# Four attention layers on one core: key sums, parts of the row maxima and late roots given to other engines

## The chip, the core and the metric

The kernel runs on one core of a Trainium2 chip. A core has TensorE (PE in the rows; its weight loads are PEld), VectorE (DVE), ScalarE (ACT), GpSimd (POOL), and SyncE (SP), which issues most DMAs. The engines run their own instruction streams and meet at semaphores: an instruction may wait until a counter has reached a value, and raises one when it ends. The metric is the device time of the kernel in microseconds (us), lower is better.

## The reference

One activation x of 16 batches x 128 x 256 goes through four layers in turn. What matters here, cut from the code:

```
L0: two cross-attentions (16 heads of 128) with layer norms, then a feed forward
L1: q = Wq x + bq;  k = Wk kv + bk;  v = Wv kv + bv;  attn = softmax(where(kv_mask, q k, -inf))
    mean = attn v;  std = sqrt(relu(attn v*v - mean*mean))
    xn = (x*m - sum(x*m)/n_valid) / sqrt(relu(var) + 1e-5);  out = (xn * std + mean) * m
L2: masked self-attention, masked cross-attention, feed forward with gelu, each with a layer norm
L3: q = layer_norm((x + pos)^T);  kv = layer_norm((ctx + pos)^T)
    r = softmax(Q K^T / sqrt(8)) V Wo + q
    out = (gelu(layer_norm(r) W1 + b1) W2 + b2 + r)^T
```

L1 and L3 have 16 heads over 256 queries and 256 keys for each batch, so that one head has a score matrix of 256 x 256.

## The kernel before

The program is one block with a stream for each engine, written by hand. Each layer is a function that exists once for every engine. In order of time: layer 0 (`wide`), feed forward 0, layer 1, layer 2, feed forward 1, layer 3 and its last feed forward (`feed_forward3`).

**Packed attention.** Layers 1 and 3 run the same code, `attention(third, ...)`, in windows, one for each batch n, and each window has 16 steps j, one for each head. A window works on several batches: the core of batch n (exponentials and weighted sums), the scores and row maxima of batch n+1 (`following`), the projections of n+2 (`ahead`), the keys and norms of n+3 (`coming`) and, in layer 3, the row statistics of batch n+4 (`fourth`). Steps that all engines take in each window:

- TensorE makes the scores of a head (L1074) for the next batch; VectorE takes their maximum over the keys, negated (`tensor_reduce`, L2106, 16 a window). The scores of head j wait for the reduce of head j-3.
- After 8 heads the maxima are brought to the rows of the next matmuls: each is split into a rounded part and a rest (`split_maxima`, L2067 and L2068), the parts are transposed by TensorE (`turn_maxima`, L1054), VectorE copies the result (`copy_maxima`, L2074) and DMAs put it behind the queries. The first half of batch n+1 is turned at j=9, the second half of batch n at j=1.
- TensorE makes the shifted scores of batch n (L1083), ScalarE their exponentials (L1672), TensorE the sums with the values (L1103).

TensorE's stream is in order, so the turn stands in front of the heads that follow:

```
pe.wait_ge(s.max_split, 2 * m + half + 1)
pe.transpose(spare[quad[0], 0:P], max_parts[half]..., ident[:, :]).then_inc(s.max_turned, 1)
```

VectorE's copy stands in front of the reduce of head 9 and waits for this transpose. Late in the window, at j=13, TensorE puts the queries of the batch after in place (`put`, L1061), and waits there for VectorE's copy of the values (`v_taken`, L2379, j=12).

**Layer 1's keys.** GpSimd casts the mask of a batch (L2612). VectorE sums the masked keys with one pass that also writes the product (L2169) and multiplies the sum by one over the valid count (L2173, `key_mean`). GpSimd subtracts the mean (L2630), multiplies by the mask (L2631), and adds the mean (L2643) into `keys_in`, which the projection of the keys reads (L1122).

**Layer 3's norms.** VectorE aggregates the statistics of 4 groups of rows (L2396, step j=6). GpSimd makes the inverse root from them by Newton's method in 14 instructions, each of which waits for the one before it (L2687, L2688, then L2690 to L2693 three times), and normalizes with four `tensor_scalar` (L2697). It then adds the positions to the rows of later batches (L2674, L2676). GpSimd does this root in 13 windows, i = -1 to 11 where i counts layer 3's batches; the first three batches are done by VectorE.

**Feed forward.** VectorE's loop over 8 rounds makes the low part of the hidden layer (`hidden_lows`, L2020), the low part of the next input (`input_low`, L2014), the norm of the one after (`norm`) and adds. In feed forward 1 `begin_last` (L2321 to L2326) stands ahead of that loop: it scales layer 3's query weights and fills the two buffers `vn`, and raises `packed_ready`.

**Last feed forward.** VectorE takes statistics of 8 groups of rows, makes their inverse root in 11 instructions (L266 to L272), and normalizes (`normalize3`, L2419), in 4 turns.

Of the kernel before, what the change touches and what calls it, by code (L numbers as in the profile page):

```python
# [152 lines left out]
class Packed:  # L153
# [3 lines left out]
    def __init__(self, sem, name):  # L157
# [32 lines left out]
        self.key_summed = sem(f"{name}_key_summed")  # L190
# [34 lines left out]
SQUARES = (9, 11)  # L225
PLACED_ROWS, TURNED_BACK, HEADS = (9, 10), (13, 14), (13, 14)
# [7 lines left out]
RSTD_STEPS = 2 + 3 * 4  # L234
# [255 lines left out]
def program(nc, t, out, outer):  # L490
# [12 lines left out]
    minus_half = sbuf(outer, "minus_half", [P, 4])  # L503
# [153 lines left out]
    scratch_keys, scratch_values = hidden[:, 4, :], hidden[:, 5, :]  # L657
# [139 lines left out]
    block = outer.enter_context(nc.Block())  # L797

# [626 lines left out]
    def _(act):  # L1425
# [179 lines left out]
        def attention(third, q_bias, k_bias, when, conclude=None):  # L1605
# [11 lines left out]
            def window(n, at, u=None):  # L1617
# [3 lines left out]
                for j in range(HN):  # L1621
# [46 lines left out]
                    if core:  # L1668
# [121 lines left out]
    def _(dve):  # L1790
# [203 lines left out]
        def feed_forward(which, bias):  # L1994
# [53 lines left out]
        def attention(third, q_bias, k_bias, when, release, own, conclude):  # L2048
# [11 lines left out]
            def split_maxima(m, half):  # L2060

                parts = max_parts[half]
                whole = maxima[half][:, :, :, :].rearrange("p a g w -> p a (g w)")
                after(dve, s.max_turned, 2 * m + half - 1)
                dve.wait_ge(s.max_ready, HN * m + HALF_HEADS * (half + 1))
                chain = Chain(dve, s.prep_chain, 2 * m + half)
                chain.link(dve.tensor_copy(parts[:, :, 0, :], whole))  # L2067
                dve.tensor_tensor(parts[:, :, 1, :], whole, parts[:, :, 0, :].bitcast(F32), ALU.subtract).then_inc(s.max_split, 1)  # L2068
# [7 lines left out]
            def window(n, at, u=None):  # L2076
                u = n % SLOTS if u is None else u
                core, following, carry, ahead = (at(i) is not None for i in (0, 1, -1, 2))
                for j in range(HN):
                    if core and j == TURN_MAXIMA[1] - 1:  # L2080
# [10 lines left out]
                    if following and j == TURN_MAXIMA[0] - 1 and third:  # L2091
                        split_maxima(n + 1, 0)
# [24 lines left out]
        def layer1():  # L2117
# [41 lines left out]
            def own(n, at, u, j):  # L2159
                following, carry, ahead, coming = (at(i) is not None for i in (1, -1, 2, 3))  # L2160
# [3 lines left out]
                if coming and j == 3:  # L2164
                    dve.wait_ge(s.loaded[1 - u], pair_turn(0, at(3), 1 - u))
                    after(dve, s.in_ready, n + 3)
                    dve.wait_ge(s.keys_chain, 3 * (n + 3) + 1)
# [741 lines left out]
```

## Time and profile before

| | us |
|---|---|
| median of 3 runs | 2293.92 (2293.31 to 2295.13) |
| the profiled execution: its own time | 2298.61 |
| the profiled execution: span of the trace | 2296.9 |
| TensorE busy | 2171.5 (95%) |
| VectorE busy | 1563.9 (68%) |
| ScalarE busy | 1574.0 (69%) |
| GpSimd busy | 739.7 (32%) |

Layer 0 takes up to about 1100 us, feed forward 0 to 1170, layer 1 to 1458 (a window of 16.5 us), layer 2 to 1841, feed forward 1 from 1847 to 1960, layer 3 from 1961 to 2257 (a window of 17.0 us), its last phase from 2246 to the end. The granted clock is at 0.9 or more of full speed in most of the 40 slices of the page. The busy time of TensorE includes time in which a matmul stands in the pipeline, so that a share near 100% does not mean that no instruction waits. In a timeline each row is one instruction, or some of one kind in a row: start, busy time, engine, line, operation, output and inputs, and in brackets how long the engine was idle before and what released it.

### The profile page before, as it was taken

To read this page: it belongs to the slowest core of one execution; us is meant where nothing else is said; L and a number is where in the kernel's file an instruction comes from. 1 tells how busy PE (TensorE), PEld (TensorE's weight loads), DVE (VectorE), ACT (ScalarE), POOL (GpSimd) and SP (SyncE) were. 2 spreads that over 40 slices of the span, in tenths; PEclk is the share of its full clock that TensorE was granted. 3 is DMA by queue.
4 is the path that set the end of the run, shared out by engine and by line. 5 is a ranking of instruction groups with operands and counts; after the bars stand their busy time and mean duration, and the time that the engine had idled before them with its cause. 6 is when DMAs were issued, how large, how long until landed. Compare 5 with 4: busy or idle time off the path is not lost. (4 is left out here: it accounts for less than half of the span.)

```text
span 2296.9 us, 51674 instructions
## 1 busy us (share of the span) xinstructions
PE 2171.5 (95%) x17289; PEld 1762.8 (77%) x17289; DVE 1563.9 (68%) x3980; ACT 1574.0 (69%) x4478; POOL 739.7 (32%) x1037
## 2 busy tenths in 40 slices
PE   6999999999999999997989999789999989899998
PEld 5899999998999999997975666456666679666664
DVE  6655555557555555557658999687777666799986
ACT  4666666665667667665737777577778866488874
POOL 2211111123211111103024655377777620344310
PEclk9999999999999999999979999799999999799999
DMA  5101112010001000002000000100000000000001
GB/s 134 24 24 24 24 24 60 24 24 1 24 24 24 24 24 24 1 1 73 0 8 10 12 9 6 38 8 1 6 17 19 10 8 6 6 10 11 8 4 38
DMA packets 72943, 47.12 MB, mean 21 GB/s; under 512 B 29232, under 2 KB 71600, under 8 KB 72752
## 3 DMA queue, kind: packets, MB, share of 16 engines
q1 hardware_dynamic: 70288, 43.30, 7.2%
q8 instruction: 114, 1.87, 0.3%
q10 hardware_dynamic: 2464, 1.32, 0.3%
q14 instruction: 77, 0.63, 0.1%
HBM read 41.45 MB, written 2.10 MB: 19 GB/s over the span
## 5 line engine op out<-in xcount | busy, mean ns | idle before, releaser
L2106 DVE TENSOR_REDUCE maxima<-bank 128x2 f32<-128x512 f32 x512 | 332.8, 681 | 34.7 <-PE bank L1083 32.3
L1672 ACT ACTIVATE probs_t<-bank 128x512 f32<-128x512 f32 x512 | 282.5, 601 | 67.2 <-PE bank L1074 66.0
L1966 DVE SCALAR_TENSOR_TENSOR wide_heads_low<-bank,wide_columns,wide_heads_high 128x128 fp32r<-128x128 f32 x512 | 155.7, 346 | 210.1 <-ACT wide_heads_high L1537 210.1
L1525 ACT ACTIVATE wide_probs<-bank,wide_neg_max 128x129 f32<-128x129 f32 x512 | 184.2, 365 | 117.7 <-DVE wide_neg_max L1946 113.4
L2461 POOL TENSOR_TENSOR wide_columns<-wide_pair_columns,zero 128x8 f32<-128x8 f32 x16 | 3.4, 210 | 648.7 <-DVE x L1979 638.8
L1520 ACT ACTIVATE wide_probs_t<-bank 128x256 f32<-128x256 f32 x256 | 98.4, 384 | 161.7 <-PE bank L945 159.7
L1950 DVE RECIPROCAL wide_inverse<-wide_sums 128x2 f32<-128x2 f32 x256 | 42.4, 166 | 227.8 <-ACT wide_probs L1525 227.8
L1531 ACT ACTIVATE wide_probs<-wide_probs,wide_inverse 128x128 f32<-128x128 f32 x448 | 156.0, 396 | 52.0 <-DVE wide_inverse L1950 52.0
L1083 PE MATMUL bank<-k_packed,q_packed 32*128 32x256 f32 x1024 | 176.5, 344 | 3.7 <-ACT q_packed L1657 2.2
L1074 PE MATMUL bank<-q_packed,k_packed 32*128 32x256 f32 x1024 | 170.8, 337 | 8.3 <-ACT probs_t L1672 7.6
L1709 ACT ACTIVATE probs<-scores_masked,neg_max 128x128 f32<-128x128 f32 x512 | 163.2, 394 | 10.6 <-DVE neg_max L2285 9.8
L959 PEld LDWEIGHTS bank<-wide_probs_t,wide_v 128*128 128x128 f32 x1024 | 148.0, 190 | 26.3 <-ACT wide_probs_t L1520 10.1
L1074 PEld LDWEIGHTS bank<-q_packed,k_packed 32*128 32x128 f32 x1024 | 107.0, 190 | 77.1 <-ACT probs_t L1672 39.3
L803 PE MATMUL bank<-wide_weights_high,wide_heads_high 128*128 128x256 f32 x512 | 166.0, 324 | 0.0
L959 PE MATMUL bank<-wide_probs_t,wide_v 128*128 128x128 f32 x1024 | 157.1, 276 | 4.8 <-ACT wide_probs_t L1520 4.7
L935 PE MATMUL bank<-wide_k,wide_q 128*128 128x129 f32 x1024 | 156.1, 275 | 2.1 <-POOL wide_normed_low L2487 1.6
L1537 ACT ACTIVATE wide_heads_high<-bank,wide_columns 128x128 fp32r<-128x128 f32 x512 | 155.4, 353 | 1.5 <-PE bank L959 0.8
L803 PE MATMUL bank<-wide_weights_high,wide_ctx_high 128*128 128x256 f32 x512 | 148.2, 289 | 0.0
L935 PEld LDWEIGHTS bank<-wide_k,wide_q 128*128 128x128 f32 x1024 | 139.9, 190 | 8.7 <-POOL wide_normed_low L2487 2.2
L805 PE MATMUL bank<-wide_weights_high,wide_heads_low 128*128 128x256 f32 x512 | 144.4, 282 | 0.0
L804 PE MATMUL bank<-wide_weights_low,wide_heads_high 128*128 128x256 f32 x512 | 144.3, 282 | 0.0
L1103 PE MATMUL bank<-probs_t,vn 128*32 128x256 f32 x2048 | 143.0, 398 | 1.2 <-DVE max_rows L2074 0.6
(316 smaller groups left out, 6794.5 us busy)
## 6 DMA issues: line engine op xcount, KB each, us to landing
cn<-in_ctx SPq DMA_DIRECT2D x48, 128.0 KB, 2.1
q_packed<-max_rows SPq DMA_DIRECT2D x256, 4.0 KB
wide_pair_weights<-in_L_xattn_wq SPq DMA_DIRECT2D x15, 256.0 KB, 2.8
wide_pair_weights<-in_L_xattn_wk SPq DMA_DIRECT2D x15, 256.0 KB, 3.1
wide_pair_weights<-in_L_xattn_wv SPq DMA_DIRECT2D x15, 256.0 KB, 3.7
wide_pair_weights<-in_L_xattn_wo SPq DMA_DIRECT2D x15, 256.0 KB, 3.5
x<-in_x SPq DMA_DIRECT2D x4, 512.0 KB, 10.3
wide_ctx_rows<-in_ctx SPq DMA_DIRECT2D x4, 512.0 KB, 8.8
```

The source lines that it names most:

```text
L803: pe.matmul(acc, wh, mh, start=start, stop=False)
L935: last = pe.matmul(wide_scores[b % 2][:, h * KEYS0:(h + 1) * KEYS0], q0[k % 2][:, h, b * P:(b + 1) * P], k0[k % 2][:, h, b, :], start=True ...
L959: last = pe.matmul(wide_heads[a % 2][:, h * P:(h + 1) * P], v0[parity][:, a, h * P:(h + 1) * P], probs_t0[:, a, h, :], start=True, stop=True)
L1074: last = pe.matmul(shifted_bank[j % 2][:, c * D:(c + 1) * D], k_packed[u][quad[a], pack, c * P:(c + 1) * P], q_packed[u][quad[a], pack, :] ...
L1083: last = pe.matmul(head_scores[packed_scores(1 - u, j)][:, c * D:(c + 1) * D], q_packed[1 - u][quad[b], pack, c * P:(c + 1) * P], k_packed ...
L1525: last = act.activation(probs0[:, b, h, :], wide_scores[b % 2][:, h * KEYS0:(h + 1) * KEYS0], ACT.Exp, bias=neg_max0[:, b, h:h + 1], accum ...
L1531: last = act.activation(probs0[:, b, h, 0:P], probs0[:, b, h, 0:P], ACT.Copy, scale=inverse0[:, b, h:h + 1])
L1537: last = act.activation(heads_high[:, h, a, :], wide_heads[a % 2][:, h * P:(h + 1) * P], ACT.Identity, bias=columns[slot][:, 3, h:h + 1])
L1672: act.activation(probs_t[j % 8][:, :], shifted_bank[j % 2][:, :], ACT.Exp, bias=0.0).then_inc(s.exp_ready, 1)
L1709: last = act.activation(probs[t][:, part], scores_masked[t][:, part], ACT.Exp, bias=neg_max[t][:, h:h + 1])
L1966: last = dve.scalar_tensor_tensor(heads_low[:, h, a, :], wide_heads[a % 2][:, h * P:(h + 1) * P], columns[slot][:, 3, h:h + 1], heads_high ...
L2106: dve.tensor_reduce(maxima[pack // 2][:, b, pack % 2, :], head_scores[packed_scores(1 - u, j)][:, :].rearrange("p (a k) -> p a k", a=UNITS ...
```

## The change

- **Layer 1's key sum.** VectorE's product with sum and its multiplication are gone. GpSimd multiplies keys and mask (`masked_keys`) right behind the cast of the mask; ScalarE runs `masked_keys` through an Identity with the scale one over the valid count and an accumulated sum, at j=4, behind the exponentials of that step. GpSimd's three steps that follow become two: (mask - 1) * mean, and `masked_keys` less that.
- **Layer 3's maxima.** `split_maxima` leaves VectorE. GpSimd takes the second half of batch n as the first thing in its window, and the first half of batch n+1 behind the root and the first of the four `tensor_scalar` of the norm, or where the window has no root, by itself.
- **Layer 3's root** on GpSimd becomes an addition and one power over 128x4.
- **Last phase.** VectorE's root over 128x8 becomes an addition on VectorE and a power on GpSimd (`roots3`), for which VectorE waits ahead of `normalize3`.
- **Feed forward.** The first round of VectorE's loop is written out ahead of it, in both feed forwards of this form, and `begin_last` stands behind that round.

```diff
+KEY_MEAN = 4
-RSTD_STEPS = 2 + 3 * 4
+RSTD_STEPS = 2
-    minus_half = sbuf(outer, "minus_half", [P, 4])
+    minus_half = sbuf(outer, "minus_half", [P, 8])
+    def parts_of_maxima(engine, m, half, apart=False):
+        s = packed
+        parts = max_parts[half]
+        whole = maxima[half][:, :, :, :].rearrange("p a g w -> p a (g w)")
+        after(engine, s.max_turned, 2 * m + half - 1)
+        engine.wait_ge(s.max_ready, HN * m + HALF_HEADS * (half + 1))
+        if apart:
+            engine.sem_inc(idle, 1)
+        chain = Chain(engine, s.prep_chain, 2 * m + half)
+        chain.link(engine.tensor_copy(parts[:, :, 0, :], whole))
+        engine.tensor_tensor(parts[:, :, 1, :], whole, parts[:, :, 0, :].bitcast(F32), ALU.subtract).then_inc(s.max_split, 1)
@@ ScalarE, attention, behind the exponential of step j
+                    if coming and not third and j == KEY_MEAN:
+                        if isinstance(n, int):
+                            act.wait_ge(packed_ready, 2)
+                        act.wait_ge(s.keys_masked, n + 4)
+                        act.activation(scratch_keys, masked_keys, ACT.Identity, scale=valid[:, ds(at(3), 1)],
+                                       accum_out=key_mean[:, 0:1]).then_inc(s.key_mean, 1)
@@ VectorE, feed forward
             input_low(0)
             norm(1)
+            hidden_lows(0)
+            input_low(1)
+            norm(2)
+            add(0)
             if which:
                 begin_last()
-            with dve.Fori(0, ROUNDS - 2) as i:
+            with dve.Fori(1, ROUNDS - 2) as i:
@@ VectorE, attention
-                    if core and j == TURN_MAXIMA[1] - 1:
+                    if core and j == TURN_MAXIMA[1] - 1 and not third:
                         split_maxima(n, 1)
-                    if following and j == TURN_MAXIMA[0] - 1 and third:
-                        split_maxima(n + 1, 0)
-                    dve.tensor_tensor_reduce(scratch_keys, cn[1 - u][:, :], mask_row[:, 0, :], 1.0, 0.0, ALU.mult, ALU.add, key_sum[:, 0:1])\
-                       .then_inc(s.key_summed, 1)
-                    dve.tensor_tensor(key_mean[:, :], key_sum[:, :], valid[:, ds(at(3), 1)], ALU.mult).then_inc(s.key_mean, 1)
@@ VectorE, last phase
-            row_statistics(dve, chain, [bank[h][:, m * P:(m + 1) * P] for h in range(SLOTS) for m in range(4)], stats3, idle)
+            moments(dve, chain, [bank[h][:, m * P:(m + 1) * P] for h in range(SLOTS) for m in range(4)], stats3, idle)
+            dve.tensor_scalar(stats3.shifted[:, :], stats3.mean_var[:, :, 1], EPS, None, ALU.add).then_inc(ff.chain, ROOT_STEPS)
+            dve.wait_ge(n2.root_ready, 2 * B + r + 1)
@@ GpSimd, layer 1
-                    keys.mark(pool.tensor_copy(mask_row[:, 0, :], row(mask_bytes, at(3))))
+                    keys.link(pool.tensor_copy(mask_row[:, 0, :], row(mask_bytes, at(3))))
+                    pool.wait_ge(s.loaded[1 - u], pair_turn(0, at(3), 1 - u))
+                    pool.tensor_tensor(masked_keys, cn[1 - u][:, :], mask_row[:, 0, :], ALU.mult).then_inc(s.keys_masked, 1)
-                    keys.link(pool.tensor_scalar(scratch_keys, cn[1 - u][:, :], key_mean[:, 0:1], None, ALU.subtract))
-                    keys.link(pool.tensor_tensor(scratch_keys, scratch_keys, mask_row[:, 0, :], ALU.mult))
+                    keys.link(pool.tensor_scalar(scratch_keys, mask_row[:, 0, :], ones[:, 0:1], key_mean[:, 0:1], ALU.subtract, ALU.mult))
-                    pool.tensor_scalar(keys_in[1 - u], scratch_keys, key_mean[:, 0:1], None, ALU.add).then_inc(s.in_ready, 1)
+                    pool.tensor_tensor(keys_in[1 - u], masked_keys, scratch_keys, ALU.subtract).then_inc(s.in_ready, 1)
@@ GpSimd, layer 3
+                if core:
+                    parts_of_maxima(pool, n, 1, True)
                     step(pool.tensor_scalar(shifted, stats.mean_var[:, :, 1], EPS, None, ALU.add))
-                    step(pool.tensor_scalar(rstd.bitcast(I32), shifted.bitcast(I32), -0.5, 1597463007.0, ALU.mult, ALU.add))
-                    for _ in range(3):
-                        step(pool.tensor_tensor(work, rstd, rstd, ALU.mult))
-                        step(pool.tensor_tensor(work, work, shifted, ALU.mult))
-                        step(pool.tensor_scalar(work, work, -0.5, 1.5, ALU.mult, ALU.add))
-                        step(pool.tensor_tensor(rstd, rstd, work, ALU.mult))
+                    step(pool.tensor_tensor(rstd, shifted, minus_half[:, 0:4], ALU.pow))
                     for k in range(4):
                         ins = pool.tensor_scalar(norm_packed[u]..., ALU.subtract, ALU.mult)
+                        if following and k == 0:
+                            parts_of_maxima(pool, n + 1, 0, True)
                     ins.then_inc(s.rows_normed, 1)
+                elif following:
+                    parts_of_maxima(pool, n + 1, 0, True)
+        def roots3():
+            norm_two = 2 * SLOTS + ROOT_STEPS
+            for r in range(TURNS3):
+                pool.wait_ge(ff.chain, 2 * ROUNDS * (norm_two + 1) + (statistics_steps(8) + 6) * r + statistics_steps(8))
+                pool.tensor_tensor(stats3.rstd[:, :], stats3.shifted[:, :], minus_half[:, :], ALU.pow).then_inc(n2.root_ready, 1)
```

GpSimd's order in a window of layer 3, before the change (`mean_var` are the statistics, `rstd` the inverse root, `w_qkv` is the memory that holds the rows; L2690 to L2693 come three times, of which one stands here):

```order
L2687 TENSOR_SCALAR stat_shifted<-mean_var 128x4
L2688 TENSOR_SCALAR rstd<-stat_shifted 128x4
L2690 TENSOR_TENSOR stat_work<-rstd 128x4
L2691 TENSOR_TENSOR stat_work<-stat_work,stat_shifted 128x4
L2692 TENSOR_SCALAR stat_work<-stat_work 128x4
L2693 TENSOR_TENSOR rstd<-rstd,stat_work 128x4
...
L2697 TENSOR_SCALAR w_qkv<-w_qkv,mean_var,rstd 128x128 x4
L2674 TENSOR_TENSOR w_qkv<-x,positions 128x256
L2676 TENSOR_TENSOR w_qkv<-cn,positions 128x256
```

And in the changed kernel, where L810 and L811 are the parts of the maxima:

```order
L810 CAST max_parts<-maxima 128x4x4
L811 TENSOR_TENSOR max_parts<-maxima,max_parts 128x4x4
L2685 TENSOR_TENSOR w_qkv<-x,positions 128x256
L2687 TENSOR_TENSOR w_qkv<-cn,positions 128x256
L2698 TENSOR_SCALAR stat_shifted<-mean_var 128x4
L2699 TENSOR_TENSOR rstd<-stat_shifted,minus_half 128x4
L2703 TENSOR_SCALAR w_qkv<-w_qkv,mean_var,rstd 128x128
L810 CAST max_parts<-maxima 128x4x4
L811 TENSOR_TENSOR max_parts<-maxima,max_parts 128x4x4
L2703 TENSOR_SCALAR w_qkv<-w_qkv,mean_var,rstd 128x128 x3
```

The 14 steps have become two, and the parts of the first half of the next batch, on which the turn waits, stand behind the power and one norm step. VectorE's order around this turn was:

```order
L2396 BN_AGGR mean_var<-stat_sums 128x2 x4
L2057 TENSOR_TENSOR k_low<-bank,k_high 128x256
L2106 TENSOR_REDUCE maxima<-bank 128x2
L2374 RECIPROCAL inverse<-bank 128x16
L2045 TENSOR_TENSOR heads_out<-bank,inverse 128x128
L2067 CAST max_parts<-maxima 128x4x4
L2068 TENSOR_TENSOR max_parts<-maxima,max_parts 128x4x4
L2106 TENSOR_REDUCE maxima<-bank 128x2
L2074 CAST max_rows<-bank 32x128
L2106 TENSOR_REDUCE maxima<-bank 128x2
```

In the changed kernel the same stretch of VectorE, by its new line numbers, is:

```order
L2402 BN_AGGR mean_var<-stat_sums 128x2 x4
L2081 TENSOR_TENSOR k_low<-bank,k_high 128x256
L2122 TENSOR_REDUCE maxima<-bank 128x2
L2380 RECIPROCAL inverse<-bank 128x16
L2069 TENSOR_TENSOR heads_out<-bank,inverse 128x128
L2122 TENSOR_REDUCE maxima<-bank 128x2
L2092 CAST max_rows<-bank 32x128
L2122 TENSOR_REDUCE maxima<-bank 128x2
```

The two rows that make the parts are gone from between the reduces of head 7 and head 8, and the copy (L2092) keeps its place. At the start of feed forward 1, VectorE's rows were, with the loop's branch as the fifth:

```order
L1815 TENSOR_SCALAR norm_rows<-x,mean_var,rstd 128x256 x2
L1824 TENSOR_TENSOR x<-x,row_bias 128x512
L2321 TENSOR_SCALAR w_queries<-w 128x128
L2323 MEMSET vn 128x1024 x2
L2326 MEMSET vn 128x32 x2
L2026 UNCONDITIONAL_BRANCH
L2026 ISA
L2020 TENSOR_TENSOR hidden_low<-hidden,hidden_high 128x512
```

Now the low parts follow the norm at once, and the fill comes behind the round's end:

```order
L1844 TENSOR_TENSOR x<-x,row_bias 128x512
L2040 TENSOR_TENSOR hidden_low<-hidden,hidden_high 128x512 x4
L2034 TENSOR_TENSOR hidden_in_low<-hidden_in,hidden_in_high 128x512
L1822 BN_STATS stat_sums<-x 128x6 x2
...
L1844 TENSOR_TENSOR x<-x,row_bias 128x512
L2029 TENSOR_TENSOR x<-x,bank 128x512
L2327 TENSOR_SCALAR w_queries<-w 128x128
L2329 MEMSET vn 128x1024 x2
L2332 MEMSET vn 128x32 x2
```

The scaling and the four fills, which stood ahead of the first low parts, are now behind the whole first round.

## Rows read from the trace of the kernel before

**Rows 1.** Busy time by stretch: us, PE, PEld, DVE, ACT, POOL, PEclk, DMA share, GB/s.

```profile
2057.17:2074.13 16.96, 16.52 (x175) 10.80 (x175) 15.60 (x40) 13.59 (x30) 7.30 (x21) 1.00 0.03 10
```

**Rows 2.** Waits of layer 3's windows (1987 to 2260 us): total, times, longest.

```profile
POOL stat_shifted L2687 <- DVE mean_var L2396: 84.4, 12, 8.4
PEld bank L1074 <- ACT probs_t L1672: 20.0, 66, 0.7
```

**Rows 3.** Timeline of GpSimd in one window of layer 3.

```profile
2064.27 0.23 POOL L2687 TENSOR_SCALAR stat_shifted<-mean_var 128x4 f32<-128x4 f32 x1 [6.88 <-DVE mean_var L2396]
2069.86 3.15 POOL L2697 TENSOR_SCALAR w_qkv<-w_qkv,mean_var,rstd 128x128 f32<-128x128 f32 x4 [0.37 <-POOL rstd L2693]
```

**Rows 4.** Timeline of VectorE, same window.

```profile
2056.08 0.66 DVE L2068 TENSOR_TENSOR max_parts<-maxima,max_parts 128x16 fp32r<-128x16 f32 x1
2063.70 0.37 DVE L2396 BATCH_NORM_AGGREGATE mean_var<-stat_sums 128x2 f32<-128x6 f32 x4
2064.29 0.68 DVE L2106 TENSOR_REDUCE maxima<-bank 128x2 f32<-128x512 f32 x1
2065.58 0.18 DVE L2068 TENSOR_TENSOR max_parts<-maxima,max_parts 128x16 fp32r<-128x16 f32 x1
2066.42 0.28 DVE L2074 CAST max_rows<-bank 32x128 fp32r<-32x128 f32 x1
2068.90 0.41 DVE L2379 COPY vn<-bank 128x256 f32<-128x256 f32 x1
```

**Rows 5.** Timeline of TensorE, same window.

```profile
2066.01 0.27 PE L1054 MATMUL bank<-ident,max_parts 128*32 128x128 f32 x1
2069.48 0.38 PE L1061 MATMUL bank<-q_high,place 128*128 128x256 f32 x1
```

**Rows 6.** Lines of GpSimd: two powers and a 128x16 product (ns min/median/max).

```profile
L2474 POOL TENSOR_TENSOR rstd<-stat_shifted,minus_half x8: 1007/1018/1048, 8.6 to 566.2; 128x4 f32<-128x4 f32 x8
L2734 POOL TENSOR_TENSOR rstd<-stat_shifted,minus_half x16: 706/710/813, 1478.3 to 1785.0; 128x2 f32<-128x2 f32 x16
L2653 POOL TENSOR_TENSOR vn<-ones,mask_keys x32: 217/223/231, 1197.4 to 1446.9; 128x16 f32<-128x16 f32 x32
```

**Rows 7.** Timelines of GpSimd and TensorE in layer 3's window 0.

```profile
1996.86 0.23 POOL L2687 TENSOR_SCALAR stat_shifted<-mean_var 128x4 f32<-128x4 f32 x1 [8.39 <-DVE mean_var L2396]
1998.36 0.27 PE L1054 MATMUL bank<-ident,max_parts 128*32 128x128 f32 x1
```

**Rows 8.** Feed forward 1's start: timelines of VectorE and TensorE, then busy time.

```profile
1861.81 0.23 DVE L2321 TENSOR_SCALAR w_queries<-w 128x128 f32<-128x128 f32 x1
1864.76 2.50 DVE L2020 TENSOR_TENSOR hidden_low<-hidden,hidden_high 128x512 fp32r<-128x512 f32 x4 [0.34 <-DVE vn L2326]
1865.60 0.55 PE L803 MATMUL bank<-w_high,hidden_high 128*128 128x256 f32 x1 [3.69 <-DVE hidden_low L2020]
1865.60:1870.90 5.30, 5.30 (x25) 5.30 (x26) 4.80 (x18) 0.28 (x1) 0.00 (x0) 0.50 0.01 3
1870.90:1873.80 2.90, 2.90 (x25) 2.90 (x25) 1.59 (x4) 0.00 (x0) 0.00 (x0) 0.97 0.00 0
```

**Rows 9.** Layer 1: timelines of VectorE, ScalarE and TensorE; an accumulator's line.

```profile
1305.55 0.98 DVE L2169 CUSTOM_DVE_ANT_0 hidden<-cn,hidden 128x256 f32<-128x256 f32 x1
1306.21 0.47 ACT L1612 ACTIVATE q_high<-bank,bias 128x256 fp32r<-128x256 f32 x1
1312.09 0.50 PE L1083 MATMUL bank<-k_packed,q_packed 32*128 32x256 f32 x2
1178.19 1.22 PE L1122 MATMUL bank<-x,w_queries 128*128 128x256 f32 x2 [4.79 <-POOL hidden L2643]
L1525 ACT ACTIVATION_READ_ACCUMULATOR wide_probs<-bank,wide_neg_max x512: 190/198/209, 42.8 to 1059.4; 128x1 f32 x171
```

**Rows 10.** Timeline of VectorE in the last phase.

```profile
2270.74 0.17 DVE L266 TENSOR_SCALAR stat_shifted<-mean_var 128x8 f32<-128x8 f32 x1
2272.96 1.37 DVE L2419 TENSOR_SCALAR norm<-bank,mean_var,rstd 128x128 f32<-128x128 f32 x4
```

More of the change, by code:

```diff
@@ L656, in program @@
     mask_row = hidden[:, 0:3, :]
-    scratch_keys, scratch_values = hidden[:, 4, :], hidden[:, 5, :]
+    masked_keys, scratch_keys, scratch_values = (hidden[:, 3 + k, :] for k in range(3))
     keys_in = [hidden[:, 6 + u, :] for u in range(SLOTS)]
@@ L2060, in split_maxima @@
             def split_maxima(m, half):
[L2062 to L2068, printed above, removed]
+                parts_of_maxima(dve, m, half)
             def copy_maxima(m, half):
@@ L2159, in own @@
             def own(n, at, u, j):
-                following, carry, ahead, coming = (at(i) is not None for i in (1, -1, 2, 3))
+                following, carry = (at(i) is not None for i in (1, -1))
                 for unit in range(UNITS):
@@ L2163, in own @@
                         weighted(unit, heads_out[unit][:, P:2 * P], unit_sums(unit)[:, :, 8:16]).then_inc(s.heads_taken, 1)
[L2164 to L2167, printed above, removed]
-                    dve.sem_inc(idle, 1)
-                    dve.tensor_tensor_reduce(scratch_keys, cn[1 - u][:, :], mask_row[:, 0, :], 1.0, 0.0, ALU.mult, ALU.add, key_sum[:, 0:1])\
-                       .then_inc(s.key_summed, 1)
-                if coming and j == 4:
-                    dve.wait_ge(s.key_summed, n + 4)
-                    dve.tensor_tensor(key_mean[:, :], key_sum[:, :], valid[:, ds(at(3), 1)], ALU.mult).then_inc(s.key_mean, 1)
                 if following and j == 6:
@@ L2473, in root @@
             pool.wait_ge(split_chain, root_steps(r) + 2 * GROUP + 1)
-            pool.tensor_tensor(stats.rstd[:, :], stats.shifted[:, :], minus_half[:, :], ALU.pow).then_inc(preparation_steps, 1)
+            pool.tensor_tensor(stats.rstd[:, :], stats.shifted[:, :], minus_half[:, 0:GROUP], ALU.pow).then_inc(preparation_steps, 1)
         def second_bias(g, half):
@@ L2607, in row @@
                     return tile[:, ds(b, 1), :].rearrange("p a d -> p (a d)")
-                keys = Chain(pool, s.keys_chain, 3 * (n + 3))
+                keys = Chain(pool, s.keys_chain, 2 * (n + 3))
                 if coming:
                     after(pool, s.in_ready, n + 3)
-                    keys.mark(pool.tensor_copy(mask_row[:, 0, :], row(mask_bytes, at(3))))
+                    keys.link(pool.tensor_copy(mask_row[:, 0, :], row(mask_bytes, at(3))))
+                    pool.wait_ge(s.loaded[1 - u], pair_turn(0, at(3), 1 - u))
+                    pool.tensor_tensor(masked_keys, cn[1 - u][:, :], mask_row[:, 0, :], ALU.mult).then_inc(s.keys_masked, 1)
                 parts = Chain(pool, s.vn_chain, 5 * (n + 1))
@@ L2665, in window @@
                 i = n - B
-                fourth, fifth = (at(o) is not None for o in (4, 5))
+                core, following, fourth, fifth = (at(o) is not None for o in (0, 1, 4, 5))
+                if core:
+                    parts_of_maxima(pool, n, 1, True)
                 if isinstance(i, int) and i < 0:
@@ L2678, in window @@
                     chain = Chain(pool, s.rstd_ready, (ROOT_STEPS + 3) * FIRST_ROWS + RSTD_STEPS * (i + 4 - FIRST_ROWS))
-                    rstd, shifted, work = stats.rstd[:, :], stats.shifted[:, :], stats.work[:, :]
+                    rstd, shifted = stats.rstd[:, :], stats.shifted[:, :]
                     def step(instruction):
@@ L2748, in _ @@
         packed_rows()
+        roots3()
     @block.sync
```

2 lines of the change are left out of this document (1 added, 1 removed).

## The prediction

> **What bounds the kernel now.** I read the share of each engine first, then the windows of layer 3, then its waits, and last the timelines around the instructions that the diff touches. No engine bounds the whole; each stage has its own cycle. In a steady window of layer 3 TensorE shows 16.52 of 16.96 us busy, VectorE 15.60, ScalarE 13.59, GpSimd 7.30 [rows 1]. The reader is to see that only 0.44 us of the window is free of TensorE, so that work taken from another engine can return 0.44 at most, while a wait put in front of TensorE is paid in full, unless TensorE's busy time hides waits. Some is hidden: its weight loads wait for ScalarE's exponentials 66 times, 20.0 us in all [rows 2], and a loop that passes from engine to engine isn't shortened when one member is relieved.
>
> GpSimd looks idle in layer 3, but its idle time ends at one place: it waits for VectorE's aggregation before each root, 84.4 us in 12 windows [rows 2]. In the window shown the aggregation runs 2063.70 to 2064.07, and the root begins 0.20 later, at 2064.27 [rows 3, 4]. TensorE's turn of the maxima for the next batch, which from now on needs GpSimd, comes at 2066.01 [rows 5]: 1.74 us after the root begins. That is the place on which the sum turns.
>
> **Layer 3, cost.** The old root has 14 steps from 2064.27 to 2069.86, 0.40 each, half of it a gap of 0.20 between linked instructions [rows 3]. The new path is: addition 2064.27 to 2064.50; gap 0.20; power over 128x4, for which layer 0 shows 1.02 [rows 6], to 2065.72; the gap before the norm, 0.37 [rows 3]; the first of four norm steps, 3.15 / 4 = 0.79 [rows 3], to 2066.88; cast 0.22, gap 0.20, rest 0.22, both by a 128x16 product of GpSimd [rows 6], to 2067.52. VectorE's rest before ended at 2065.76 and the turn came 0.25 behind it [rows 4, 5], so now at 2067.77, about 1.7 us late. The maxima themselves are ready in time: the reduce of head 7 ends at 2064.97 [rows 4].
>
> Who stands behind the turn: on TensorE, in order, the heads from 10 on; on VectorE the copy at 2066.42 [rows 4] and behind it the reduce of head 9, without which TensorE's scores of head 12 don't start; through them the copy of the values at 2068.90 [rows 4] and the put of the queries at 2069.48 [rows 5]. VectorE has 0.36 less to do before (the parts between the reduces of heads 7 and 8), which doesn't help, since it waits for the turn. At the window's start it loses about 1.0 of work more: the cast and the rest that ends at 2056.74 [rows 4]. The rest took 0.66 there and 0.18 in mid window [rows 4]. That relief comes where TensorE has its 0.44 at most. I take 0.3 of it: 1.7 - 0.3 = 1.4 us a window, in 11 windows 15.4.
>
> In window 0 the root begins at 1996.86 and the turn stood at 1998.36 [rows 7], 1.50 apart instead of 1.74, so 2.0 late, less 0.3: 1.7; the window before it, in which the first root of GpSimd runs, I take alike, 3.4 for both. The three windows at the end have no root, and GpSimd is free; at most 0.3 each is gained, which I leave out. Layer 3: +18.8. Bounds for the 13 windows: below, the power at the 0.71 of the 128x2 one [rows 6] and all of the 0.44 used, 1.7 - 0.31 - 0.44 = 0.95, +12.4; above, nothing recovered and 0.2 more for a slower link, +24.7.
>
> The nearest prices of the same step on the two engines are 0.22 on GpSimd [rows 6] and 0.18 on VectorE [rows 4], both for 128x16. The Trainium skill, "GPSIMD Engine Reference", section 4.1, says that an elementwise operation with two inputs is to go to VectorE, since GpSimd takes about twice as long. By that rule the subtraction would be an estimated 0.36, the turn 0.14 later, and layer 3 +20.6; the row at this size shows far less, and the order of GpSimd's queue, not its speed, makes the sum.
>
> **Feed forward 1.** VectorE begins `begin_last` at 1861.81 and gets to the low parts at 1864.76; TensorE's first matmul comes at 1865.60 after 3.69 idle [rows 8]. With the fill behind the round this is 2.95 us earlier, and nothing else is shown to be late there: -3.0. Then the clock: from 1865.60 25 matmul records take 5.30 us at a granted clock of 0.50 (1.2 GHz), and the next 25 take 2.90 at 0.97 (2.4 GHz) [rows 8]; the engine had been idle 3.69 before it fell. With an idle time of some 0.7 it may not fall: up to 5.30 - 2.90 = 2.4 more, of which I take 1.9. Against it, the fill, 2.95 of VectorE's time, now stands behind the first round and may delay the second round: 0 to 0.8, I take 0.4. Together -4.5, bounds -2.4 and -5.3. The same edit in feed forward 0 has no fill and only unrolls a round: nothing.
>
> **Layer 1.** VectorE's product with sum ran 0.98 at 1305.55 [rows 9] while its next reduce had no scores yet; it fits into a hole and saves nearly nothing. ScalarE gets a pass over 128x256, 0.47 as for `q_high`, and the reading of the accumulator, about 0.20 [rows 9]: 0.65, placed in a stretch in which ScalarE works without a break, just ahead of the exponentials on which heads 6 and 7 of TensorE wait. TensorE has slack behind it: its shifted scores at 1312.09 [rows 9] come only when a reduce of VectorE lets the scores beside them go, so the delay of about 0.6 ends in that wait. In the steady windows I take nothing. GpSimd's product is done before the sum needs it, and it has two steps instead of three behind the mean, which shortens the chain to the projection by one. That chain is on the path once, at the layer's start, where TensorE waited 4.79 us for `keys_in` [rows 9]: one pass over 128x256 and its gap less, of the kind of a fourth of L2697's 3.15 for half the columns [rows 3], -1.2; and -0.3 for the rest. Layer 1: -1.5. Bounds: all of the 0.6 paid in 15 windows, +9; or VectorE's whole relief of 0.98 felt in 13 windows, -13.
>
> **Last phase.** The root runs 2270.74 to 2272.96, 2.22 us [rows 10], on VectorE's own cycle. Now: addition 0.17, 0.20 to GpSimd, a power over 128x8, and about 0.15 back. From 0.71 for 2 columns and 1.02 for 4 [rows 6] 8 columns make 1.02 + 2 x 0.31 = 1.64 by a straight line, together 2.16 to 2.30: four turns at about +0.05, +0.2. If the power grows with nothing it is 1.02 and -2.5; if it doubles with its columns 2.04 and +1.8.
>
> **The sum.** 18.8 - 4.5 - 1.5 + 0.2 = +13.0. The profiled execution has a span of 2296.9 and an own time of 2298.61, 4.7 above the median of the runs; its durations are applied as differences, so the forecast stands on the median: 2293.9 + 13.0 = 2307.
>
> **Rivals.**
> - *GpSimd is in time, or the path recovers (faster).* If the way from aggregation to turn took no longer than the 1.94 us that it has (2064.07 to 2066.01 [rows 4, 5]) instead of 3.7, only the relief is left: 0.44 in 16 windows, -7, with -4.5 and -1.5 it gives 2281. It decides where layer 3's loss per window falls below 5.8 / 13 = 0.45 us, since feed forward 1, layer 1 and the last phase give 5.8. For it speaks that weight loads wait 20.0 us for exponentials [rows 2], so TensorE's 16.52 isn't all work. The rest at the window's start that took 0.66 instead of 0.18 [rows 4] shows that GpSimd and VectorE hinder one another, so that VectorE's relief could be the larger one. Against it stands that the turn is in order ahead of both engines' next heads. The Trainium skill, "Advanced Engine Details and Errata", VectorE Performance Modes, says that VectorE's second port is shared with GpSimd; by it the 0.48 comes back, but GpSimd's new steps would in turn hold VectorE up. Chance 0.16.
> - *The late turn is mostly absorbed.* 0.5 us a window, +6.5, against -5.8: 2294.6. Chance 0.09.
> - *ScalarE's sum is not absorbed in layer 1.* 0.6 in 15 windows more, +9: 2316. For it speaks the place in ScalarE's unbroken stretch; against it the wait at 1312.09. Chance 0.09.
> - *The forecast*, 2299 to 2314: chance 0.66.
>
> **Numbers.** What a measurement of this kernel can tell from no change is about 0.2%, 4.6 us. Slower takes the forecast and most of the third rival, 0.74; same takes the second, 0.09; faster the first and a little of the second, 0.17. The likeliest case gives 2307. The range goes down to 2290, which leaves out most of the first rival, and up to 2317, which takes in the third.
>
> **What would show it.** In layer 3 with a root, the turn (L1054's successor) about 1.7 us later behind the aggregation than before, an idle VectorE before the copy of the maxima, released by the turn, and a window of 18.3 to 18.4 instead of 16.96 us; the last three windows as before. Feed forward 1: TensorE's 3.69 us idle down to under 1, and the clock at 0.97 through the first round. Layer 1: a window of 16.5 us, and TensorE's wait for the keys at its start 1 us shorter. Last phase: a power of 1.4 to 1.8 us and VectorE idle for it. The prediction is wrong if the window of layer 3 stays below 17.4, which would say that the turn has slack that the rows don't show, or if layer 1's window grows.

## The result and the profile after

The changed kernel takes 2321.56 us (median of 4 runs, 2317.48 to 2322.9) against 2294.53 for the kernel before; the ratio is 1.0114 with a 95% interval of 1.0101 to 1.0126. It is slower by 26 us (27 by the two medians), twice the +13 that was forecast, and outside the range. The sign and the place were right. A second cost behind the first, a fall of TensorE's clock, had been left out.

Windows of layer 3 in the changed kernel, each from one first-half turn to the next (columns as in [rows 1]), then the stretch behind the last turn, then the start of feed forward 1:

```profile
2029.24:2049.03 19.79, 18.19 (x175) 11.60 (x175) 14.71 (x35) 13.72 (x29) 6.62 (x13) 0.91 0.03 11
2049.03:2069.00 19.97, 18.27 (x174) 11.81 (x175) 14.71 (x35) 13.77 (x29) 6.62 (x13) 0.91 0.03 8
2069.00:2087.24 18.24, 16.64 (x174) 10.84 (x175) 14.52 (x35) 13.73 (x29) 6.62 (x13) 1.00 0.03 9
2258.79:2274.40 15.61, 14.87 (x103) 8.53 (x105) 3.88 (x24) 9.48 (x20) 1.66 (x1) 0.67 0.01 3
1856.00:1870.00 14.00, 13.27 (x111) 13.06 (x111) 12.32 (x39) 9.18 (x19) 1.53 (x3) 1.00 0.01 1
```

There are two kinds of windows. The short one shown takes 18.24 us at a granted clock of 1.00 (the short ones in the steady part 18.0 to 18.5), within 0.1 of the 18.3 that was forecast. The long ones, 19.7 to 20.0, take about 1.6 us more, hold the same number of matmuls, and their mean clock is 0.91. That column, not the first, tells what makes them long.

GpSimd, VectorE and TensorE around the turn of one window (timelines; the first three rows are GpSimd's addition, power and first norm step, the next two the parts):

```profile
2065.78 0.23 POOL L2698 TENSOR_SCALAR stat_shifted<-mean_var 128x4 f32<-128x4 f32 x1 [6.30 <-DVE mean_var L2402]
2066.19 1.04 POOL L2699 TENSOR_TENSOR rstd<-stat_shifted,minus_half 128x4 f32<-128x4 f32 x1 [0.18 <-POOL stat_shifted L2698]
2067.60 0.80 POOL L2703 TENSOR_SCALAR w_qkv<-w_qkv,mean_var,rstd 128x128 f32<-128x128 f32 x1 [0.37 <-POOL rstd L2699]
2068.35 0.20 POOL L810 CAST max_parts<-maxima 128x16 fp32r<-128x16 f32 x1
2068.63 0.22 POOL L811 TENSOR_TENSOR max_parts<-maxima,max_parts 128x16 fp32r<-128x16 f32 x1
2069.00 0.27 PE L1068 MATMUL bank<-ident,max_parts 128*32 128x128 f32 x1 [1.32 <-POOL max_parts L811]
2069.40 0.28 DVE L2092 CAST max_rows<-bank 32x128 fp32r<-32x128 f32 x1 [1.83 <-PE bank L1068]
```

The turn comes 3.22 us behind the root's start instead of 1.74 [rows 3, 5]; TensorE stands 1.32 us for GpSimd, VectorE 1.83 us for TensorE. In the waits of the windows (total, times, longest) the new entries are:

```profile
PE bank L1068 <- POOL max_parts L811: 17.0, 12, 2.3
DVE max_rows L2092 <- PE bank L1068: 24.0, 22, 2.2
```

What then happens in a long window, and in a short one, on TensorE (timelines, the same instructions just behind the turn at 2049.03 and behind the one at 2069.00):

```profile
2049.85 1.73 PE L1117 MATMUL bank<-probs_t,vn 128*32 128x256 f32 x16
2051.51 1.22 PE L1189 MATMUL bank<-w,hidden 128*128 128x128 f32 x4
2052.75 0.41 PE L1075 MATMUL bank<-k_low,place 128*128 128x256 f32 x1
...
2069.87 1.07 PE L1117 MATMUL bank<-probs_t,vn 128*32 128x256 f32 x16
2070.87 0.71 PE L1189 MATMUL bank<-w,hidden 128*128 128x128 f32 x4
2071.54 0.28 PE L1075 MATMUL bank<-k_low,place 128*128 128x256 f32 x1
```

The same 16 matmuls take 1.73 instead of 1.07 us. After the gap the clock fell from 2.4 to 1.2 GHz and stayed there for 3 to 4 us: for 2049.50 to 2053.50 the granted clock is 0.58, for 2069.50 to 2072.00 it is 1.00.

Where the 23.2 us between the two spans (2296.9 and 2320.1) lie, read from the starts of all 32 turns of layer 3 in both traces:

| stretch | before | after | difference |
|---|---|---|---|
| start to the first turn of layer 3 | 1979.62 | 1973.93 | -5.7 |
| second-half turn to next first-half turn, 12 with a root between them | 7.66 to 8.32 | 9.05 to 9.36 | +16.6 |
| the same, the last 3, without a root | 6.84 to 7.19 | 6.66 to 7.00 | -0.6 |
| first-half turn to second-half turn, 16 windows | 8.9 to 9.2 in the steady ones | 8.6 to 9.1, and 10.4 to 10.7 in 7 of them | +10.0 |
| last turn to the end | 58.4 | 61.3 | +2.9 |

The first four rows make -5.7 + 26.0, the last +2.9. The last row has two parts in it: the kernels below with the same last phase need 57.7 us there, so the low clock costs 3.6, and the last phase's edit gives back 0.7.

### The profile page after: what moved, and what is told of

Its sections match the earlier page's. It is cut to its first block and busy times, and to the rows that moved or that the text cites. A ratio compares the mean times of both kernels' runs of the same rounds, so it can differ in the third digit from the quotient of the medians.

```text
span 2320.1 us, 51190 instructions
## 1 busy us (share of the span) xinstructions
PE 2177.0 (94%) x17289; PEld 1764.7 (76%) x17289; DVE 1534.8 (66%) x3828; ACT 1580.4 (68%) x4510; POOL 739.9 (32%) x949
## 3 DMA queue, kind: packets, MB, share of 16 engines
q10 hardware_dynamic: 2464, 1.32, 0.3%
```

## The experiments

The theory at this point: **(1)** the turn of the maxima waits for GpSimd's queue, 1.4 us a window; **(2)** the gap that this makes on TensorE lowers its clock in some windows, 1.5 us each time, and perhaps once more in the last phase, where the row above shows 0.67. The rivals: GpSimd's new steps hinder VectorE; the long windows have another cause, such as what is late behind the turn (the DMAs that place the maxima).

**Parts on VectorE again** (`a_parts_vector`), the rest as changed:

```diff
-                    if core and j == TURN_MAXIMA[1] - 1 and not third:
+                    if core and j == TURN_MAXIMA[1] - 1:
                         split_maxima(n, 1)
...
-                if core:
-                    parts_of_maxima(pool, n, 1, True)
...
-                        if following and k == 0:
-                            parts_of_maxima(pool, n + 1, 0, True)
-                elif following:
-                    parts_of_maxima(pool, n + 1, 0, True)
...
+                    if following and j == TURN_MAXIMA[0] - 1 and third:
+                        split_maxima(n + 1, 0)
```

> The changed kernel with both halves of layer 3's maxima parts made by VectorE again; all else (power root, layer 1's sum, feed forward, last phase) as changed. Theory (the turn that waits for GpSimd costs about 1.4 us in each of 12 windows, and the gap it makes in TensorE's work brings the granted clock down to half in 7 windows for 1.5 us each, and once more after the last window for 2.9): layer 3's window goes back to 16.9 us, the clock there to 1.00, and the time to 2321.6 - 16 - 10 - 3 = 2292 or a few us less, 2288 to 2293. Rival 1 (the long windows come from the power or the norm steps on GpSimd hindering VectorE, not from the turn): the window stays at 18 to 20 us and the time above 2310. Rival 2 (only the late turn costs, the clock falls for another reason): about 2305, with windows at a clock of 0.91 left.

Measured: 2292.47 us, ratio to the kernel before 0.999 (0.9981 to 1.0). The power root and all other parts of the change are in it, and 29.1 us of the changed kernel are gone, as the theory asked (2288 to 2293); both rivals, above 2310 and about 2305, fall. Its steady windows take 17.0 and 16.9 us, and 11 of them together (busy time by stretch):

```profile
1991.55:2176.92 185.37, 180.64 (x1907) 117.76 (x1906) 169.28 (x426) 150.23 (x319) 62.22 (x86) 1.00 0.03 10
```

The clock is 1.00, and the last turn is followed by 57.7 us instead of 61.3: the detour of the last phase's root was not what cost there, the clock was.

**First half ahead of the root** (`b_ahead_of_root`). GpSimd keeps both halves, but makes the first half's parts before it waits for the aggregation:

```diff
+                if following:
+                    parts_of_maxima(pool, n + 1, 0, True)
                 if fourth and not (isinstance(i, int) and i + 4 < FIRST_ROWS):
...
-                        if following and k == 0:
-                            parts_of_maxima(pool, n + 1, 0, True)
-                elif following:
-                    parts_of_maxima(pool, n + 1, 0, True)
```

> The changed kernel with the first half's parts on GpSimd ahead of the root's wait instead of behind the power and one norm step. Theory: the place in GpSimd's queue is the cause, not the engine. The reduce of head 7 ends about 0.9 us after the aggregation, the parts take 0.65 on GpSimd, so the turn comes at most 0.2 us later than on VectorE; the clock stays at 1.00 and the time is 2286 to 2293, equal to the kernel with parts on VectorE or a little under it. Rival (GpSimd's parts themselves are too slow or hinder VectorE): 2300 or more. Second rival: the root behind the parts becomes late for the transposes at j=13, window 17.5 us or more.

Measured: 2288.26 us, ratio 0.9975 (0.9964 to 0.9986): the fastest kernel of the study. On GpSimd's timeline the parts stand ahead of the root, and TensorE's turn follows in time:

```profile
2057.31 0.20 POOL L810 CAST max_parts<-maxima 128x16 fp32r<-128x16 f32 x1 [7.20 <-DVE maxima L2122]
2057.59 0.22 POOL L811 TENSOR_TENSOR max_parts<-maxima,max_parts 128x16 fp32r<-128x16 f32 x1
2057.79 0.23 POOL L2700 TENSOR_SCALAR stat_shifted<-mean_var 128x4 f32<-128x4 f32 x1
2058.18 0.27 PE L1068 MATMUL bank<-ident,max_parts 128*32 128x128 f32 x1
```

So neither the engine nor the speed of its two instructions was the fault, but their place in its queue. The same 11 windows:

```profile
1990.99:2175.77 184.78, 179.30 (x1907) 116.41 (x1906) 158.70 (x382) 150.14 (x319) 71.31 (x130) 1.00 0.03 10
```

VectorE is busy 158.70 instead of 169.28 us, 10.6 less, and the stretch is shorter by 0.6. In the traces the relief that the change brings is worth 0.05 us a window, far under the 0.44 of the first rival and the 0.3 of my sum. The medians of the plain runs stand 4.2 us apart (2292.47 and 2288.26), the two profiled executions 1.4; the rest is not placed, and the intervals of the two ratios overlap, so a relief somewhat larger than the trace shows isn't excluded.

**Behind two norm steps** (`c_two_steps`): `k == 0` becomes `k == 1`, one more norm step ahead of the parts.

> The changed kernel with the first half's parts behind two norm steps of GpSimd instead of one: 0.79 us more wait at the turn. Theory (late turn plus clock): each of 12 windows grows by 0.8 through the wait, and the gap of about 2.1 us brings the clock down in every window instead of 7 of 12: 2321.6 + 10 + up to 8 = 2332 to 2340. Rival (the turn's wait is covered in part by slack, and the long windows are a matter of odd and even): less than +6, 2327 or less.

Measured: 2337.09 us, ratio 1.019 (1.0173 to 1.0207). From second-half to next first-half turn 9.98 to 10.15 us, 0.79 more than in the changed kernel. All but one of the 12 windows with a root have more than 10 us from first-half to second-half turn, some 11.4 to 11.95, one 9.1. The time lies in the range that the theory gave, 2332 to 2340. The clock over 1993 to 2222 us:

```profile
1993.00:2222.00 229.00, 200.28 (x1906) 129.30 (x1906) 160.65 (x382) 151.18 (x318) 72.54 (x133) 0.90 0.03 8
```

Behind its last turn this trace has 57.7 us (2278.33 to 2336.0) and no low clock, so the fall that the changed kernel shows there doesn't come from the last phase's own edit. Nor do the rows show a gap that would explain it. Here are the 9.93 us from the last first-half turn to the fall, in the changed kernel and then in this one:

```profile
2251.81:2261.74 9.93, 9.16 (x96) 5.04 (x93) 6.45 (x14) 7.20 (x16) 0.42 (x2) 1.00 0.01 2
2271.35:2281.28 9.93, 9.17 (x96) 5.04 (x93) 6.44 (x14) 7.19 (x16) 0.42 (x2) 1.00 0.01 2
```

TensorE does the same in both, and no idle time of it before the fall is longer than 0.5 us; yet in the changed kernel the clock then falls for 10 us, and here it stays up. Why it fell there is open.

**The gap filled** (`d_filled`). TensorE gets work that nobody needs, in front of the wait:

```diff
                 def turn_maxima(m, half):
+                    if third and half == 0:
+                        for _ in range(10):
+                            pe.transpose(spare[quad[0], 0:P], ident[:, 0:32], ident[:, :])
```

> The changed kernel with 10 transposes of the identity (32 columns each, into the place that the turn writes next) on TensorE ahead of each wait of a first half's turn in layer 3: about 1.3 us of work that nobody needs, in the gap of 1.3. Theory (the gap lowers the clock): the clock stays at 1.00, all windows take 18.2 to 18.5 us, none 19.8, and the time falls by 8 to 13 us to 2309 to 2314 although work is added. Rival (the clock falls for another reason, or the long windows aren't the clock's): the time rises by 1 to 13 us, since the added work comes on top where the gap is shorter than the work.

Measured: 2304.45 us, ratio 1.0048 (1.0031 to 1.0064): with more work 17.1 us less than the changed kernel (15 by the two ratios to the kernel before), more than the 8 to 13 expected. TensorE's timeline shows the fill and the turn, and the busy time of the windows with a root the clock:

```profile
2059.19 1.25 PE L1069 MATMUL bank<-ident 128*32 128x128 f32 x10
2060.59 0.28 PE L1071 MATMUL bank<-ident,max_parts 128*32 128x128 f32 x1
```

```profile
1988.00:2205.00 217.00, 210.15 (x2197) 138.69 (x2197) 172.54 (x409) 163.61 (x345) 74.78 (x138) 1.00 0.03 9
```

All intervals from first-half to second-half turn are 9.1 or less, those from second half to first half stay at 9.1 to 9.3 in the windows with a root (9.96 behind the first): the delay is still there, the clock's share is gone. In its trace the way from the first turn to the end is 14.9 us shorter than in the changed kernel: -14.6 behind first-half turns, of which 2.7 in the first window, whose clock was low before the change too; +3.2 where the fill stands without a gap; -3.6 behind the last turn. The expectation had left out the first window. The two spans differ by 18.1; the other 3.3 lie ahead of layer 3's first turn, where the two kernels are alike.

**The longer gap filled** (`k_two_steps_filled`): the two-step kernel with 16 such transposes.

> The kernel with parts behind two norm steps, and 16 transposes of the identity on TensorE ahead of each first half's turn in layer 3, for its gap of 2.1 us. Without them it took 2337.1 us, with 12 windows of which 11 held a stretch at half clock. Theory: the late turn remains (10.0 from second-half to first-half turn) but the clock stays up and all intervals from first-half to second-half turn are 9.1: 2337 - 11 x 1.5 - 3 = 2317, less what the fill costs in the last three windows (+4) = 2314 to 2322. Rival (the long intervals come from what is late behind the turn, such as the DMAs that place the maxima, and the filling of the first kernel worked by its own place): 2330 or more.

Measured: 2318.48 us, ratio 1.0098 (1.0081 to 1.0115), 18.6 under the same kernel without them (21 by the ratios) and in the range that was expected. The late turn stays (9.87 to 10.04), the intervals behind it are 8.6 to 9.1, and the clock over 1993 to 2222 us is:

```profile
1993.00:2222.00 229.00, 220.37 (x2299) 147.13 (x2300) 174.69 (x415) 164.95 (x348) 74.18 (x139) 1.00 0.03 8
```

The DMAs that place the maxima begin 0.6 to 0.8 us behind the turn here, as they do without the fill and before the change, and with the turn they are as late as without the fill; the rival that blamed what is late behind the turn falls.

**Behind the root, ahead of all norm steps** (`j_ahead_of_norm`):

> The changed kernel with the first half's parts behind the root but ahead of all four norm steps: the wait at the turn is 0.79 us shorter than in the changed kernel. Measured so far per window from one second-half turn to the next first-half turn: 7.8 us with parts ahead of the root, 9.2 to 9.35 in the changed kernel, 10.0 to 10.15 one step later. Theory: 8.4 to 8.6 here, a gap of about 0.5 us on TensorE, the clock at 1.00 in every window, 9.1 from first-half to second-half turn everywhere, and 2288 + 12 x 0.65 = 2294 to 2298. Rival (the clock falls at any gap here): some windows with 10.5 and a time above 2300.

Measured: 2300.76 us, ratio 1.0025 (1.0015 to 1.0034), 2.8 us above the range expected. The intervals from second half to first half are 8.5 to 8.8 in the steady windows, 0.2 more than expected, the clock 1.00 but for one window, the last with a root (10.4 us). Ahead of that window's turn TensorE had waited longer than at any other:

```profile
2186.32 0.27 PE L1068 MATMUL bank<-ident,max_parts 128*32 128x128 f32 x1 [1.36 <-POOL max_parts L811]
```

At the other eleven it waits 0.5 to 1.15 us, and behind none of them does the clock fall: the rival, that it falls at any gap here, holds for none of the short ones.

The four places of the two parts in GpSimd's queue, read from the intervals of the turns:

| place | second to first half, us | TensorE waits for GpSimd, us (mean of 12) | windows with a low clock | median, us |
|---|---|---|---|---|
| ahead of the root | 7.8 | once, 0.4 | none of 12 | 2288.3 |
| behind the root | 8.7 | 0.80 | 1 of 12 | 2300.8 |
| behind one norm step (the change) | 9.2 | 1.42 | 7 of 12 | 2321.6 |
| behind two | 10.0 | 2.13 | 11 of 12 | 2337.1 |

(The first window, in which the clock is low at least in part in all four and before, is not counted among the twelve. The medians come from different sessions, in which the kernel before took 2294.4 to 2295.5.)

**The other parts alone.** The feed forward's edit alone on the kernel before (`f_first_round_only`), the diff as in the change:

> The kernel before with the feed forward's edit alone (first round written out, the fill of layer 3's buffers behind it). In profiled executions the start of feed forward 1 gained 3.0 us of TensorE's wait and its clock stayed up for another 2.4, so the profile is expected to show 5.4 us less between the first round and layer 3. Theory: the plain runs gain the same, 2289.0. Rival: plain runs gain only a part (1 to 3 us), since the kernel with the parts on VectorE, which has this edit too, was only 2 us under the one before.

Measured: 2290.46 us, ratio 0.9988 (0.9977 to 0.9999), -2.8 us with an interval of -5.3 to -0.2; the median of the kernel before in the same session is 2295.3, 4.8 above. In its trace the way from the norm of round 1 to the last add is 93.9 us against 99.2 before, so the profiled gain is 5.4; the interval of the plain runs reaches it only with its end. Theory and rival are not told apart.

Layer 1's key sum alone on the kernel before (`g_key_sum_only`):

> The kernel before with layer 1's key sum alone moved to GpSimd and ScalarE. Theory (the pass on ScalarE, 0.65, ends in TensorE's slack; 1.3 us less wait at the layer's start): 2293, within 0.2% of the kernel before. Rival (ScalarE's pass delays heads 6 and 7 each window): slower by up to 9. Second rival (VectorE's relief of 0.98 in 13 windows is felt): faster by up to 13.

Measured: 2296.05 us, ratio 1.0007 (0.9998 to 1.0016): no difference. TensorE waits 3.45 instead of 4.79 us at the layer's start [rows 9], as forecast. The windows show a small gain too: from the fourth to the sixteenth first-half turn of layer 1 it is 195.4 us here, 194.8 in the changed kernel and in every other kernel with both the key sum moved and the first round written out, and 196.1 before. The plain runs don't show such amounts. One reason stands in the same traces: layer 1's first two windows, in which the clock is low in part, take 30.3 to 36.2 us over the twelve traces, and 33.7 to 36.2 in kernels that are alike there.

Two parts undone in the fastest kernel: the last phase's root on VectorE (`h_ahead_last_on_vector`), and layer 1's sum on VectorE (`i_ahead_sum_on_vector`).

> The kernel with the first half's parts ahead of the root, and the last phase's root on VectorE by Newton's method again. The power over 128x8 took 1.64 us and the whole detour about as long as the 11 steps. Theory: no difference from the kernel it is made from (2288.3), within 2 us. Rival (the power's detour costs in the last phase): 1 to 3 us faster.

> The kernel with the first half's parts ahead of the root, and layer 1's key sum on VectorE as before. If the key sum's move is worth the 1.3 us at the layer's start and no more, this is 1 to 2 us slower than 2288.3. If ScalarE's pass costs in the windows, it is faster than 2288.3 by 2 or more.

Measured: 2290.69 us, ratio 0.9982 (0.9973 to 0.9991), and 2291.25 us, ratio 0.9987 (0.9978 to 0.9996). Both stand 2 to 3 us above 2288.26, a little more than the 2 and the 1 to 2 that were expected, with intervals that overlap its own; as far as this tells, neither part costs anything. The traces put a small gain on each: behind the last turn the first has 58.75 us against 57.70, and in layer 1's windows the second has 196.2 against 194.8.

## Why the prediction was wrong

**What bounds layer 3, and the place.** Right. The sum turned on the turn of the maxima behind GpSimd's root, and the runs with the parts on VectorE or ahead of the root give back 29 and 33 us.

**The path.** Forecast: the turn 3.50 us behind the root's start, 1.7 us late. Measured in the window shown: 3.22, 1.5 late. The power took 1.04 (from 1.02), the norm step 0.80 (0.79), the parts 0.20 and 0.22 (0.22 each); the rest of the cast came 0.08 behind it instead of a gap of 0.20.

**What is paid of it.** Forecast 1.4 us a window and 18.8 in all, 17.1 without the first; measured 16.6 in the 12 intervals, 1.38 each, plus a share in the first window that can't be parted from its low clock. Nearly right, but by luck: I subtracted 0.3 for VectorE's relief, which is worth 0.05 in the traces (`b_ahead_of_root`), and the delay was 0.2 to 0.3 shorter than I had it, so that the two errors cancel.

**The step that failed.** "Who stands behind the turn" counted the engines that wait and not what TensorE's own standing still does to it. I had read that effect in feed forward 1 (3.69 us idle, then 0.50 [rows 8]) and priced it there as a gain of the change, but did not ask it of the new gap of 1.4 us in layer 3. The sum has no term for it. In the changed kernel the clock fell in 7 of 12 windows (1.3 to 1.6 us each against the same interval before, 10.2 together), and `d_filled` and `k_two_steps_filled` show that it is the gap: with it filled, and the delay left, the clock stays at 1.00. It fell once more behind the last turn, 3.6 us; that this comes from the gaps is not shown. Together they are 13.8 us, about the size of the miss. In the two profiled executions everything else comes out 3.6 us under the sum (9.4 instead of 13.0), by the other terms of this section; the plain runs are too scattered to place so little. The forecast for what would show it, "a window of 18.3 to 18.4", holds for the short windows only. The test that the prediction set for itself there, wrong if the window stays below 17.4, looked only for a turn that costs less than forecast.

**Three windows without a root.** Forecast up to 0.3 gained in each, left out; measured 0.2 each.

**Feed forward 1.** Forecast -4.5; the profile shows TensorE's wait down from 3.69 to 0.73 and the clock at 1.00 from 1856 to 1870, 5.4 us together. VectorE's fill behind the first round cost nothing that shows. In plain runs it is -2.8 by the ratio and -4.8 by the medians, not sharply measured.

**Layer 1.** Forecast -1.5, of which 1.2 at the start; `g_key_sum_only` gives no difference, +1.6 with an interval of -0.5 to +3.7, which leaves -1.5 out. The changed kernel's profile shows -1.3 at the start and another -1.3 in the windows, where I had put nothing. The two are not reconciled. ScalarE's pass took 0.50 and 0.19 as costed, and the slack on TensorE took it up. VectorE's hole stays a hole in the window shown: it is idle 1.06 us where the product with sum stood (the first row; the other two are ScalarE's pass):

```profile
1305.95 0.69 DVE L2122 TENSOR_REDUCE maxima<-bank 128x2 f32<-128x512 f32 x1 [1.06 <-PE bank L1097]
1306.40 0.50 ACT L1691 ACTIVATE hidden<-hidden,valid 128x256 f32<-128x256 f32 x1
1306.80 0.19 ACT L1691 ACTIVATION_READ_ACCUMULATOR hidden<-hidden,valid 128x1 f32 x1
```

**Last phase.** Forecast +0.2 with a power over 128x8 at 1.64, by a straight line from two rows; measured:

```profile
L2718 POOL TENSOR_TENSOR rstd<-stat_shifted,minus_half x4: 1636/1636/1657, 2272.7 to 2304.1; 128x8 f32<-128x8 f32 x4
```

The addition starts at 2284.83 and the norm at 2286.83, 2.00 us instead of 2.22 [rows 10]: the detour is 0.2 a turn shorter, where I had it 0.05 longer. From the last turn of the maxima to the end this makes -0.7 against the kernel before (57.7 and 58.4).

**The rivals.** The faster one asked for a way from aggregation to turn of at most 1.94 us. That was the right point to ask about, but its price was too high: with the way short enough (`b_ahead_of_root`) the time is 2288, not 2281, since relief of VectorE is worth next to nothing there. The second, a late turn that is mostly absorbed, fell: of 1.5 us 1.38 are paid. The slower one, ScalarE's pass, did not occur: layer 1's windows didn't grow.

## What to carry to other kernels

When a change puts a wait in front of TensorE, price it twice: the wait, and what the clock does after the gap. Here a wait of 1.4 us on average cost 1.4 and, in 7 of 12 windows, 1.5 more, so that moving two instructions of 0.2 us each past one of 0.8 on an "idle" engine (32% busy) was worth 21 us. Where an engine's share is low, read where its queue stands when the asker comes, not how busy it is; and a relief counts only on the engine that is asked for last.

## What the runs showed of the hardware

Gaps on TensorE of 1.2 to 1.3 us, two of them above 2 (mean 1.42), in windows in which it is about 91% busy, were followed by a granted clock of half for 3 to 4 us in 7 of 12 windows and not in the other 5. Gaps of 2.0 to 2.8 us were so in 11 of 12, mostly for as long, three times for twice as long. With gaps of 0.5 to 1.15 us it happened in none of 11, and once behind one of 1.36 (`j_ahead_of_norm`). The length of the gap alone doesn't decide it: in the changed kernel the longest, 2.33 us at the second first-half turn, left the clock up, and in the steady windows the falls come in a fixed order, two windows low and one spared, three times over, while the gaps there are 1.25 to 1.32 in the low windows and 1.19 to 1.32 in the spared ones. Ten transposes of 32 columns in the gap, 1.25 us of empty work, kept the clock up and made the kernel 15 to 17 us faster. The Trainium skill, "TensorE: Matmul & The Clock Gate", Part 1, "What's actually happening", describes a clock that is throttled by default and that activity of TensorE releases, and the traces agree in that: filled, the windows run at 1.00, with the gap they fall to 0.91.

GpSimd's power grows linearly with its columns at these sizes: 0.71 us for 2 [rows 6], 1.02 to 1.04 for 4, 1.64 for 8, which a straight line of 0.155 us a column and 0.4 to start fits.
